# Three-stage vision tower on one core: shared buffers between the last two stages, an earlier load of the last stage's weights, one transpose for each pair of key heads

## What is computed

```python
# stage 1, tokens: correlation with a 31 x 31 template per channel, divided by the local deviation
h = mean_over_channels(dw_conv(x, norm_template) / (sqrt(box(x*x) - box(x)**2) + 1e-9))   # [16, 256, 256]
# stage 2, attention: 256 tokens of width 256, 16 query heads, 8 key and value heads of 64
x = rmsnorm(h) * norm_w
q, k, v = l2norm(x @ Wq) * gq, l2norm(x @ Wk) * gk, x @ Wv
a = softmax(causal(tanh(q @ k.T / 50) * 50 / 8))       # query heads 2j and 2j+1 share key head j
h = layernorm(h + (a @ v summed over the two query heads of a key head) @ Wout)
# stage 3, MLP: 1024 hidden units, three hidden layers
g = silu(h @ w1.T * s1) * (h @ w2.T * s2)
g = gelu(gelu(g @ h1.T * sh1) @ h2.T * sh2)
out = layernorm(h + g @ w3.T * s3)
```

## Time and profile before

| | |
|---|---|
| median of 3 runs | 1977.88 us (1976.26 to 1985.11) |
| the profiled execution | 1977.19 us, its span 1975.5 us |
| PE busy | 1827.4 us, 93% of the span, 11768 matmuls |
| DVE busy | 1122.4 us, 57% |
| ACT, POOL busy | 870.6 us (44%), 399.7 us (20%) |
| DMA queue of SP | 94.96 MB, 13.6% of 16 engines |

### The profile page before, as it was taken

The page is one execution under the profiler, slowest core; times in us unless marked ns, Lnnn a source line. Parts: engine busy times, 40 slices in busy tenths (PEclk is TensorE's granted clock), DMA queues, the critical chain, the costliest instruction groups (busy, mean ns, idle before and its releaser), DMA issues. The chain is left out here.

```text
span 1975.5 us, 31720 instructions
## 1 busy us (share of the span) xinstructions
PE 1827.4 (93%) x11768; PEld 1578.6 (80%) x11768; DVE 1122.4 (57%) x2084; ACT 870.6 (44%) x1073; POOL 399.7 (20%) x502
## 2 busy tenths in 40 slices
PE   5899999999969989999998998699999999999997
PEld 5788998988958877877887887587878787787876
DVE  8788888887866766675775674414142331414141
ACT  4654455556426764674775575122122222212221
POOL 2000000000111211121121112233332433333342
PEclk9999999999979999999999998799999999999999
DMA  5322222214011002000200100510000000000000
GB/s 170 109 78 86 87 79 108 94 54 142 23 37 61 23 16 81 23 16 18 86 24 8 66 23 16 236 44 22 0 23 1 22 23 1 22 0 22 1 11 12
DMA packets 17308, 97.10 MB, mean 49 GB/s; under 512 B 2937, under 2 KB 3065, under 8 KB 11650
## 3 DMA queue, kind: packets, MB, share of 16 engines
q1 hardware_dynamic: 17154, 94.96, 13.6%
HBM read 82.33 MB, written 24.15 MB: 54 GB/s over the span
## 5 line engine op out<-in xcount | busy, mean ns | idle before, releaser
L556 PE MATMUL conv<-w_hi,x_hi 128*128 128x368 f16 (+5 forms) x1320 | 355.1, 279 | 7.7 <-issue 5.7
L556 PE MATMUL conv<-w_lo,x_hi 128*128 128x368 f16 (+5 forms) x1320 | 356.0, 279 | 0.0
L556 PE MATMUL conv<-w_hi,x_lo 128*128 128x368 f16 (+5 forms) x1320 | 354.6, 279 | 0.0
L1322 ACT ACTIVATE raw_c<-ring,sh 128x512 f32<-128x512 f32 x128 | 88.1, 688 | 370.2 <-PE ring L1419 370.2
L1110 PE MATMUL mixed<-v,probs 128*128 128x65 f32 x1536 | 201.3, 282 | 22.6 <-DVE parts L990 19.3
L1419 PE MATMUL ring<-ha_hi,wh 128*128 128x512 f32 x512 | 207.8, 406 | 13.0 <-POOL ha_lo L1284 13.0
L1110 PEld LDWEIGHTS mixed<-v,probs 128*128 128x128 f32 x1536 | 185.6, 195 | 37.8 <-issue 22.8
L1284 POOL TENSOR_TENSOR ha_lo<-raw_c,ha_hi 128x512 fp32r<-128x512 f32 x128 | 164.9, 1288 | 210.1 <-DVE ha_hi L1334 210.1
L556 PEld LDWEIGHTS conv<-w_hi,x_hi 128*128 128x128 f16 x1320 | 192.8, 146 | 16.7 <-issue 8.4
L1419 PE MATMUL ring<-ha_lo,wh 128*128 128x512 f32 x512 | 205.4, 401 | 0.0
L1419 PE MATMUL ring<-hb_hi,wh 128*128 128x512 f32 x512 | 202.2, 395 | 0.0
(11 more groups left out here) (148 smaller groups left out, 3472.9 us busy)
## 6 DMA issues: line engine op xcount, KB each, us to landing
xt<-x_columns_in SPq DMA_DIRECT2D x12, 1163.0 KB, 5.6
xp<-x_patches_in SPq DMA_DIRECT2D x12, 1152.0 KB, 5.1
hidden_words<-hidden_weights_in SPq DMA_DIRECT2D x8, 1408.0 KB, 9.0
words<-hidden_words SPq DMA_DIRECT2D x32, 352.0 KB, 3.1
wh<-hidden_words SPq DMA_DIRECT2D x2, 4096.0 KB, 22.0
tokens<-planes SPq DMA_DIRECT2D x4, 1024.0 KB, 4.3
lines<-tokens SPq DMA_DIRECT2D x4, 1024.0 KB, 5.5
h<-tokens SPq DMA_DIRECT2D x4, 1024.0 KB, 6.8
```

The source lines that it names most:

```text
L556: ins = pe.matmul(out, xs[:, c, RI - 1 - i:RI - 1 - i + NR, :, x].rearrange("p r g -> p (r g)"), w, start=(t == 0), stop=(t == len(terms) ...
L1322: act.activation(raw[:, u % 4], bank, ACT.Gelu, scale=scale[:, m:m + 1]).then_inc(s_gelu, 1)
```

## The change

It has six parts.

1. **Bridge.** `ident`, `neg_half`, w1, w2, the five scales, both halves of `x1_c` and the last moments become buffers that are made before the attention stage and live through the MLP. SP loads x1 (the halves of group 0), w1, w2 and the scales in `FINAL`, behind the last chunk of weight words. POOL makes `ident` and `neg_half` at the start of the attention block, in place of an unused mask.
2. **Last normalisation moved.** In `FINAL` the attention block ends with the moments. POOL's root and DVE's normalisation of the last group come at the start of the MLP block (DVE behind the two `turn_lo` of lot 0), SP stores the two halves of X1 there, and DVE waits for those stores ahead of unit 8 of each lot, because `hb` takes the place of `h`. The flag's reduction on DVE moves ahead of the last `project`.
3. **Weights in pieces.** wh1 and wh2 come in four DMAs each, of 256 columns, which is 1 KB for each k and partition; `mid1` and `mid2` wait for the piece they need.
4. **Middle layers.** Outputs 0 and 1 are computed together: k 0 to 5 of output 0, k 0 to 5 of output 1, then k 6 and 7 of each. The number of matmuls stays the same.
5. **Stores by halves.** y is worked off in two pairs of token rows: product, residual, stats and moments of pair 0 follow `down` 0, and so on; POOL takes the root of each pair; the normalisation of both comes after, and each pair has one store of 256 KB.
6. **Keys turned once.** The host reorders the query heads so that a 128-wide block holds one query head of key head 2e and one of 2e+1. A block of keys as it stands then matches, `keys` and its second copy go, one `make` step turns all eight key heads (steps 11 and 15 go), and DVE reads that bank twice, with two gammas. `mix` adds every second head, twice as wide.

```diff
-        part, rinv, total = (planes_3[:, k] for k in range(3))
+        total, part, rinv = (planes_3[:, k] for k in range(3))
...
-    [("make", 11), ("make", 7), ("scale", 1)],
+    [("make", 7), ("scale", 1)],
     [("make", 12)],
-    [("make", 13), ("make", 14), ("make", 15)],
+    [("make", 13), ("make", 14)],
...
+                if run is FINAL:
+                    for half in range(2):
+                        sp.dma_start(flat(br.x1[:, half]), X1[half]).then_inc(br.s_x1[half], 16)
+                    for k, (name, dst) in enumerate((("w1", br.w1), ("w2", br.w2))):
+                        src = WORDS[:, k * KD * HID:(k + 1) * KD * HID]
+                        sp.dma_start(flat(dst[:]).bitcast(F32), src).then_inc(br.s_w[name], 16)
+                    for dst, src in zip((br.s1, br.s2, br.sh1, br.sh2, br.s3), SCALES):
+                        sp.dma_start(dst[:], src).then_inc(br.s_scales, 16)
+                    return
...
-                if run.before:
+                if run is BODY:
                     pool.wait_ge(s_aggr, g + 1)
...
-                        dve.tensor_tensor(heads[:, 0:QH], heads[:, 0:QH], by[:, 0:QH].to_broadcast([P, QH, DH]), ALU.mult)
-                        for m in range(2):
-                            ins = dve.tensor_tensor(keys[:, tb, :, m], heads[:, QH:],
-                                                    by[:, QH:].to_broadcast([P, HEADS, DH]), ALU.mult)
-                        ins.then_inc(s_qn, 1)
+                        dve.tensor_tensor(heads, heads, by, ALU.mult).then_inc(s_qn, 1)
...
+                        for m in range(2):
+                            by = gamma[:, m::2].rearrange("p (h t) -> p h t", t=1).to_broadcast([P, EB, P])
+                            ins = dve.tensor_tensor(kt[:, img % 2, m::2, P * tb:P * tb + P], bank, by, ALU.mult)
...
-                        dve.tensor_tensor(o[:, img % 2, :, hd], parts[:, :, 0], parts[:, :, 1],
-                                          ALU.add).then_inc(s_o, 1)
+                        if hd % 2:
+                            dve.wait_ge(s_mixread, g * NH + n + 2)
+                            dve.tensor_tensor(pair, pair, parts[:], ALU.add).then_inc(s_o, 1)
...
+                        if run is FINAL and k == 0:
+                            dve.wait_ge(s_bits, GROUPS * CHUNKS + 1)
+                            dve.tensor_scalar(words[:], bits[:], 0xFFF, None, ALU.bitwise_and).then_inc(s_lows, 1)
+                            dve.wait_ge(s_lows, 1)
+                            dve.tensor_reduce(lows[:, 0:1], words[:], AX_X, ALU.max).then_inc(s_lows, 1)
...
+            def mid_weights(name, dst, first):
+                src = WORDS[:, first:first + KH * HID].rearrange("p (k c) -> p k c", k=KH)
+                for m in range(0, KH, MID_CHUNK):
+                    cols = slice(m * P, (m + MID_CHUNK) * P)
+                    sp.dma_start(dst[:, :, cols].bitcast(F32), src[:, :, cols])\
+                      .then_inc(br.s_mid[name][m // MID_CHUNK], 16)
+                    if (name, m) == ("wh1", MID_CHUNK):
+                        sp.wait_ge(s_late_norm, 1)
+                        for half in range(2):
+                            sp.dma_start(X1[2 * GROUPS - 2 + half], flat(h[:, SA * half:SA * half + SA]))\
+                              .then_inc(s_late_store, 16)
...
+            dve.wait_ge(s_late, 2)
+            for a in range(PR):
+                ins = dve.tensor_scalar(h[:, a], h[:, a], br.moments[:, a, 0:1], br.rstd[:, a:a + 1],
+                                        ALU.subtract, ALU.mult)
+            ins.then_inc(s_late_norm, 1)
...
+                dve.wait_ge(s_late_store, 32)
...
+                    dve.tensor_tensor(y[:, pair], bank, by, ALU.mult).then_inc(s_edve, 1)
+                    dve.wait_ge(s_edve, DOWN + n * DOWN + s + 1)
+                    dve.tensor_tensor(y[:, pair], y[:, pair], x1[:, parity, pair], ALU.add).then_inc(s_sum, 1)
...
+                            banks = [bank, free_bank(n, parity, (kind, 1))]
+                            for ks in (range(KH - 2), range(KH - 2, KH)):
+                                for q in range(2):
+                                    for k in ks:
+                                        if q == 0:
+                                            pe.wait_ge(s_lo, n * UNITS + first + k + 5)
+                                        ins = product(banks[q], [(w[:, k, q * P:q * P + P], (src[0][:, k], src[1][:, k]))],
+                                                      exact, k == 0)
+                                    if KH - 1 in ks:
+                                        ins.then_inc(s_job, 1)
+                            continue
```

More of the change, by code:

```diff
@@ L610, in first_order @@
     order += [("make", 0, j) for j in (4, 5, 6)] + [("scale", 0, 0), ("sum", 0, 1), ("root", 0, 1)]
-    order += [("make", 0, j) for j in (3, 7, 8, 9, 10, 11)] + [("scale", 0, 1)]
-    return order + [("make", 0, j) for j in (12, 13, 14, 15)]
+    order += [("make", 0, j) for j in (3, 7, 8, 9, 10)] + [("scale", 0, 1)]
+    return order + [("make", 0, j) for j in (12, 13, 14)]
 def attention_order(last):
@@ L1407, in turn, with product @@
                 ins.then_inc(s_job, 1)
-            def product(bank, pairs, exact):
-                start = True
+            def product(bank, pairs, exact, start=True):
                 for left, right in pairs:
@@ L1429, in lot @@
                     cols = slice(m * P, m * P + P)
+                    if (kind, m) in (("mid1", 1), ("mid2", 1)):
+                        continue
                     bank = free_bank(n, parity, step)
```

234 lines of the change are left out of this document (117 added, 117 removed).

## The result

The changed kernel takes 1900.48 us, the median of four runs (1897.83 to 1905.45), where the median of four runs of the kernel before is 1981.49 us. The ratio is 0.958, with a 95% interval of 0.954 to 0.961: 81 us faster. The profiled execution of the changed kernel took 1905.45 us, with a span of 1903.6.

The account below looks back on a forecast made before the run. The prediction took PE, busy for 93% of the span, as the bound. Attention 17, passage 12.3, middle layers 23.7 and end 3.9 us sum to 57: 1977.2 - 57 = 1920 us, 8-in-10 range 1906 to 1938.

Parts of the forecast that it names:

- the stall of `mid1`: In the MLP, six of eight first middle layers wait for POOL's low parts; curing that was to give 23.7 us.
- unit 5 and unit 7: Low parts that the first middle layer needs: forecast at 1367.6 and 1370.9 us, wanted at 1369.0 and 1372.7, so no wait.
- The passage: From attention to the MLP: PE turns tokens 11.5 us earlier, plus 0.8 without w1's wait; 12.3 us, bounds 9 to 12.6.
- POOL's root (1.66 us) runs while PE turns tokens: At the MLP's start, the moved root of the last normalisation was to be hidden under PE's turning of tokens.
- about 2 us to spare: At the MLP's start, DVE's moved normalisation ends near 1255.3 us; the first `up` product is due at 1257.4.
- more comes: Rival: MLP's first lot at full clock saves 3.4 us, attention gives another 8; 1909 us, chance 0.1.
- Attention: Attention stage: fewer key transposes 13.7 us, image 0 1.5, fewer `parts` waits 2; together 17 us, between 4 and 28.
- Image 0's chain: In attention, image 0's serial preparation, where PE waits for DVE, was to shorten by 1.5 us.
- The end: After the last matmul: the last lot's shorter chain and earlier store save 3.9 us, between 2.5 and 4.3.
- Attention did not give little: Rival: the transposes only covered PE's waits in attention, so some 3 of 17 us come; 1934 us, chance 0.13.
- The stall did not come back: Rival: part of the first middle layers' wait returns, as clock fall or wait; half the term lost, 1932 us, chance 0.15.
- The pieces never came late: Rival: wh1 and wh2 in pieces load at 58 GB/s, PE waits 89 us in the MLP; 2009 us, chance 0.02.

## Where the prediction was right, and the step that failed

**Direction and mechanisms: right.** All four places gave about what they were said to give, or more. The largest term, the stall of `mid1` (23.7 us), came in full in the six lots that had it, with unit 5 and unit 7 within 0.3 us of their forecast times.

**The step that failed** is how the sum treats a layer that never waits. The prediction says "A middle layer that never waits takes 29.74 us for its 128 matmuls, 0.232 us each", keeps that figure in "That gives 202.1 - 6 x 29.74 = 23.7 us" and expects "every `mid1` at 29.8 us", and so puts the pace of the matmuls at no change, without a reason. The pace is a property of where the buffers lie. At the new distance the same layer takes 29.02 us, in all 16 layers (lot 0's `mid1` has its wait on top): 11.7 us that are in no term. The prediction reads the diff for what each instruction does and never asks what moving the buffers does, though the bridge moves most of them.

**What else the sum put at nothing.** The idle time at the loop's two back edges (1.9 and 1.7 us in `down`, and 1.8 more in gate and up behind them, most of it at the lower clock) is 5.4 us, visible in the kernel before, and went because less code stands ahead of the loop. Against it, lot 0's `mid1` lost 1.3 us and the other gate, up and `down` steps 0.05 us each, 0.8 together. 23.7 + 11.7 + 5.4 - 1.3 - 0.8 = 38.7, the change of the MLP in the table.

**The passage: right in sum, wrong in one part.** 13.1 us came for 12.3, above the 12.6 that the prediction gave as its upper bound: the first turn of tokens began 3.3 us behind the last `project` matmul and not 4.0, in part because the way from the flag to SP took 0.5 us and not 0.85. But "POOL's root (1.66 us) runs while PE turns tokens" failed: it ran 9.5 us later, and "about 2 us to spare" on DVE became 6 us too late. The trace of before had the sign: DVE waited 2.03 us for an all-reduce of 0.4 us, though its own part of the flag was done at 1254.20, and POOL, whose root had ended at 1250.13, began it only at 1255.81. What it costs is in lot 0. The rival "more comes" asked whether lot 0 would run at full clock; it took 18.33 us again, now 1.65 of it a wait and the rest the clock.

**Attention: right in this pair of profiles, too small over all.** In the five traces here with the attention of before, the last `project` matmul comes at 1245.3 to 1251.6, 1248.4 on average; in the fifteen with the keys turned once, at 1217.0 to 1228.7, 1223.6 on average. That is 24.8 us, inside the bounds of 4 to 28, where I took 17. Image 0's chain, from the first projection matmul to the first product of q and k, gave 1.4 of them (1.5 taken). Behind it PE's idle time fell by 3.7 us (35.1 to 31.4), against 2 taken, and its busy time by 19.2 us. By the pace at full clock the 120 transposes are 13.7 of these. The other 5.5 go with the clock: between that product and the last `project` matmul PE had the lower level for 48.5 us on average before and for 31.5 after, and the sum has no term for that. The `parts` waits, 19.3 us, are 12.0 and 3.1 now. Why fewer falls of the clock follow was not tried. This is also why the median lies 5 us below the profiled execution, whose attention was the longest of the fifteen.

**The whole miss.** By the medians 81 us came for 57. The pace gives 11.7 of the missing 24, attention 7.8 on average, the back edges 5.4 and the passage 0.8; the end (0.4) and the losses of 1.3 and 0.8 go against them. That is 23.2.

**The end: right.** 3.5 us for 3.9. By the rule of the Trainium skill (SBUF — State Buffer, Who interferes with whom) that the prediction cites, a root beside DVE's work would have been held up to 0.75 us. POOL's power takes 0.71 us there and 0.72 in the half of the lot where DVE is idle, and it overlaps DVE's work for little more than 0.1 us. The price did not appear, and with so short an overlap this hardly tests the rule.

**Rivals.** Attention did not give little. The stall did not come back but for lot 0, where `mid1` waits 0.9 us for `ha_lo`, after POOL's late root. Of "more comes" the half about attention came, and the half about lot 0 did not. The pieces never came late: PE waited for no weights.

## What to carry to other kernels

When a change moves buffers, measure a stretch of matmuls that never waits in both kernels: here 128 bytes between weights and activations were worth 2.4% of the time of the wide matmuls, and the gain showed in full only after the stall behind it was cured. Time the back edges of long loops: here code ahead of a loop gave or cost it 2 to 3 us a turn. After an all-reduce on POOL, put one throwaway instruction where nobody waits, before POOL is on anybody's path: here that gave PE 3.2 us in the windows, too little for the times to tell.

## What the runs showed of the hardware

- 128 matmuls of 512 columns with their weight loads take 29.02 us when the distance in bytes between the two operands in a partition is 0 modulo 256, and 29.74 to 29.87 at 128; the 64 of gate and up take 14.53 at 0, 14.87 at 128, 14.92 at 224 and 14.93 at 96. The 256-column matmuls of `down` don't gain: 8.16 us at 0, 8.09 at 128. Other distances were not tried.
- A loop's back edge on PE costs 0.23 to 0.25 us or 3.3 to 3.9, by the place of its code; the two loops of over 2200 executed instructions always cost the latter.
- Between its MODIFY_POOL_CONFIG pair and an all-reduce POOL stands for 5.6 to 5.8 us where the input is there in time, and ahead of its first arithmetic after the all-reduce for 6.8 to 7.0 us under the last `project`, or 9.1 to 10.2 at the start of the MLP.
